# Spreading a batch's four value gathers over six units of a paged attention loop

## The chip, the cores and the metric

The kernel runs on one core of a Trainium2 chip. The time is device time of one execution, in microseconds; three runs of the kernel before give 2389.03, 2390.1 and 2392.03, median 2390.1. A profile was taken of one further execution.

## The reference

Four layers are added to `x` one after another (64 batches of 32 rows and 512 columns; the attention reads the rows as tokens): a product with a weight chosen by condition, a base weight with adapters of rank 16, an attention over a paged cache, and again a product by condition. The change lies in the third:

```python
x = x + _L0_cond_ref(x, itok_B_0_15, L0_cond_weights)
x = x + _L1_cond_ref(x, itok_B_6_15, ...)
x = x + _L2_cond_ref(x, ..., L2_cond_k_cache, L2_cond_v_cache, itok_Bx16_0_63, itok_B_207_1644)
x = x + _L3_cond_ref(x, L3_cond_weights, itok_B_0_15)
# in L2, for each batch: 32 query heads, 8 key heads of 128, 16 pages of 32 rows plus 32 own rows
kc = k_cache[block_table].reshape(bsz, L, HK, D)        # L = 512
vc = v_cache[block_table].reshape(bsz, L, HK, D)
k_all, v_all = concatenate([kc, k]), concatenate([vc, v])
scores = where(valid, einsum('bqhd,bkhd->bhqk', q, k_all) * SCALE, -1e30)
o = einsum('bhqk,bkhd->bqhd', softmax(scores), v_all)
return einsum('bse,de->bsd', o.reshape(bsz, seqlen, HQ * D), Wo)
```

## The kernel before

The attention is a loop over 512 units. A unit is one key head of one batch with its four query heads, which are stacked to 128 rows of queries against 544 keys. Eight units make a batch, 32 units (four batches) a group, and there are 16 groups. Every engine runs its own `step(g, u)` for each unit, u from 0 to 31, and the steps are staggered by semaphores.

PE, in step u, in this order: `turn_own` (u a multiple of 4), `score` of unit u+2 (six matmuls, L1209), `turn_p` of unit u (four transposes, L1092; at multiples of 4 it comes after `values`), a part of `out_proj` of the finished group (only in steps 30, 31 and 0 to 5, L1260), and `values` of unit u-1 (four products of the values with the turned probabilities, L1241, and at the last of four units the own rows, L1252). Products in fp32r are made of three: high by high, high by low, low by high.

The split of keys and queries into high and low parts is shared. ACT makes `k_hi` of unit u+4 (L715). DVE makes the first 11 of 17 slots of `k_lo`, POOL the rest (both through `k_low`, L284). POOL also makes `q_hi` (L549) and `q_lo` (L551). POOL's `split_q(n + 4)` waits until PE has scored unit n+2 (`s_qk`), as it overwrites the buffer of that unit; PE's `score` waits for `s_klo` (DVE) and `s_qp` (POOL). DVE further takes the masked maximum (L975), and normalises the probabilities (L986, L987); ACT takes the exponentials (L721) and moves the turned probabilities out of PSUM (L765).

Values come from the cache in HBM by gathers. `gather_v` (L514) is an indirect DMA issued by POOL: it fetches 128 rows of 4 KB, that is 512 KB, into one of four parts of a batch's value buffer. There are two such buffers, `v_sb[0]` and `v_sb[1]`, used by alternate batches. POOL's `step` issues the gathers of batch g*4+k+2 with (u - 10) = 8k + m, m from 0 to 3: gather m in step 10 + 8k + m, behind the `split_q` of that step. At m = 0 it first waits until the batch that used the buffer is finished (`s_po`), and copies the next batch's indices (L511). With k = -1 these are steps 2 to 5, with k = 0, 1 and 2 steps 10 to 13, 18 to 21 and 26 to 29. The first group issues batch 1's gathers in steps 2 to 5 by a line of its own. All four gathers of a buffer add to `s_v`; PE's `values` waits for 64 on it at the batch's first unit, thus in step 17 for gathers of steps 10 to 13, in step 25 for those of 18 to 21, in step 1 of the next group for those of 26 to 29, and in step 9 for those of 2 to 5.

SP issues the other loads in a fixed order per batch: own keys and queries (L359, L361) once `s_qp` says that POOL has split the buffer's last unit, then sixteen pages of K of 128 KB (L354) once `s_klo` says it for DVE, then the own values (L366), then the store of the outputs.

Of the kernel before, what the change touches and what calls it, by code (L numbers as in the profile page):

```python
# [28 lines left out]
B, C, T = 64, 32, 512  # L29
# [7 lines left out]
BT = P // C  # L37
# [13 lines left out]

WO_AT = {UG - 2: 0, UG - 1: 2, 0: 4, 1: 6, 2: 8, 3: 11, 4: 14, 5: H2}
LOW = 11
WO_SPLIT = 8

SCALE = 1.0 / float(np.sqrt(D))
# [10 lines left out]
def ge(eng, sem, val):  # L67

    if not isinstance(val, int) or val > 0:
        eng.wait_ge(sem, val)  # L70


def build(nc, x, cond_row, id_row, bt_row, idx_pages, seq_tok, seq_all, w0, w3, wb, bias,
# [3 lines left out]
    with ctx:  # L77
# [203 lines left out]
        def k_low(engine, b, h, u, slots):  # L281

            lo, hi = (k[u % 2].rearrange("p (s t) -> p s t", t=PSIZE)[:, slots, :] for k in (k_lo, k_hi))
            return engine.tensor_tensor(lo, k_sb[b][:, slots, h, :], hi.bitcast(F32), ALU.subtract)  # L284
# [199 lines left out]
        @block.gpsimd  # L484
        def _(pool):
            PL = [mybir.EngineType.Pool]
            pool.wait_ge(s_ids, 32)
            pool.wait_ge(s_la, 16)

            def pick(i, j):  # L490

                ge(pool, s_hmm, i * 4 - 3 + j)
                _, rows = nc.values_load_multi_w_load_instructions(
                    ids[0:1, bass.ds(i * 16 + 4 * j, BT)], engines=PL, min_val=0, max_val=LORAS - 1)
                for b in range(BT):
                    nc.gpsimd.tensor_copy(a4[j][:, :, b * RANK:(b + 1) * RANK],
                                          la_sb[:, bass.ds(rows[b], 1), :].rearrange("p a (c r) -> p (a c) r", c=HC))\
                        .then_inc(s_pick[j], 1)

            for j in range(4):  # L500
                pick(0, j)
            with pool.Fori(1, NT // 4) as i:
                for j in range(4):
                    pick(i, j)

            pool.wait_ge(s_x2T, NT)
            for j in range(4):
                pool.wait_ge(s_x2st[j], 16 * (NT // 4))
            def next_idx(b, k):

                nc.gpsimd.tensor_copy(idx[k][:], idx_all[:, bass.ds(b * 4, 4)]).then_inc(s_idx, 1)  # L511

            def gather_v(k, par, m):
                nc.gpsimd.indirect_dma_start(  # L514
                    out=v_sb[par][:, m, :], out_offset=None, in_=v_cache,
                    in_offset=bass.IndirectOffsetOnAxis(ap=idx[k][:, m:m + 1], axis=0)).then_inc(s_v[par], 16)

            nc.gpsimd.memset(ones[:], 1.0).then_inc(s_ones, 1)
            pool.wait_ge(s_ones, 5)
            pool.wait_ge(s_idx0, 1)  # L520
            next_idx(0, 0)
            next_idx(1, 1)
            next_idx(2, 2)
            pool.wait_ge(s_idx, 2)
            for m in range(4):
                gather_v(0, 0, m)


            def add_halves(e, t):
                pool.wait_ge(s_rot, e * NT + t + 1)  # L530
                ge(pool, s_tq, e * NT + t - 3)
                qv = qr_sb[t % 4].rearrange("p (h d) -> p h d", h=4)
                for lo, hi in ((0, HD), (HD, 0)):
                    nc.gpsimd.tensor_tensor(qv[:, :, lo:lo + HD], t1_sb[t % 2][:, :, lo:lo + HD],  # L534
                                            t2_sb[t % 2][:, :, hi:hi + HD], ALU.add).then_inc(s_qr, 1)

            for t in range(NT):
                add_halves(0, t)
            with pool.Fori(1, QKB - 1) as e:
                for t in range(NT):  # L540
                    add_halves(e, t)
            def split_q(n, u, pair):

                b, h = u // HK % 2, u % HK
                if h == 0:
                    pool.wait_ge(s_k[b], pair * KLOAD + KLOAD)
                ge(pool, s_qk, n - 1)
                q = q_sb[b][:, h * P:(h + 1) * P]
                nc.gpsimd.tensor_tensor(q_hi[u % 2], q, ones[:], ALU.mult).then_inc(s_qhi, 1)  # L549
                pool.wait_ge(s_qhi, n + 1)  # L550
                nc.gpsimd.tensor_tensor(q_lo[u % 2], q, q_hi[u % 2].bitcast(F32), ALU.subtract)  # L551
                pool.wait_ge(s_khi, n + 1)
                k_low(nc.gpsimd, b, h, u, slice(LOW, NPP + 1)).then_inc(s_qp, 1)

            def step(g, u):
                n = g * UG + u
                fixed = isinstance(n, int)
                if not (fixed and n + 4 >= NU):
                    split_q(n + 4, u + 4, g * 2 + (u + 4) // (2 * HK))

                k, m = (u - 10) // HK, (u - 10) % HK
                if m < 4 and not (fixed and not 2 <= g * BT + k + 2 < B):
                    if m == 0:
                        b = g * BT + (k + 2)
                        pool.wait_ge(s_idx, b + 1)
                        pool.wait_ge(s_po, g * (2 * BT) + 2 * (k + 1))
                        next_idx(b + 1, (k + 3) % 4)
                    gather_v((k + 2) % 4, k % 2, m)

            for t in range(NT):  # L570
                add_halves(QKB - 1, t)
                if t in (NT - 4, NT - 2):
                    u = (t - (NT - 4)) // 2
                    split_q(u, u, 0)
            for u in range(2, 4):
                split_q(u, u, 0)
            for u in range(ROT):
                step(0, u)
                if 2 <= u < 6:
                    gather_v(1, 1, u - 2)  # L580
            with pool.Fori(0, NT - 1) as g:
                for u in range(ROT, UG):
                    step(g, u)
                for u in range(ROT):
                    step(g + 1, u)
            for u in range(ROT, UG):
                step(NT - 1, u)
            pool.wait_ge(s_po, NU // 4)
            for i in range(2):
                nc.gpsimd.memset(bd3[i], 0.0).then_inc(s_zero3, 1)  # L590
# [3 lines left out]
        def _(act):  # L594
# [149 lines left out]
            def split_wo(half, h, raw):  # L744

                if h == 0:
                    act.wait_ge(s_wo_in, 16 * half + 16)
                at = slice(h * T, (h + 1) * T)
                nc.scalar.copy(wo_hi[:, at], raw[:, at]).then_inc(s_wohi, 1)

            def step(g, u):
                n = g * UG + u
                fixed = isinstance(n, int)
                if u % 4 == 0 and not (fixed and n == 0):
                    own_turned(g, u)
                if not (fixed and n + 4 >= NU):
                    split_k(n + 4, u + 4, g * 2 + (u + 4) // (2 * HK))
                if u % 4 == 0:
                    if not (fixed and n + 2 >= NU):
                        exps(n + 2, u + 2)  # L760
                    if not (fixed and n == 0):
                        out_heads(g, u)
                act.wait_ge(s_ta, n + 1)
                ge(act, s_pv, n - 1)
                nc.scalar.copy(pT_sb[u % 2], pT).then_inc(s_evA, 1)  # L765
                if u % 4 and not (fixed and n + 2 >= NU):
                    exps(n + 2, u + 2)
# [16 lines left out]
            for u in range(ROT):  # L784
                step(0, u)
                if 0 <= u - WO_SPLIT < H2:
                    split_wo(0, u - WO_SPLIT, wo_raw)
            with act.Fori(0, NT - 1) as g:
# [31 lines left out]
        def _(dve):  # L820
# [142 lines left out]
            def split_k(n, u):  # L963

                b, h = u // HK % 2, u % HK
                dve.wait_ge(s_khi, n + 1)
                k_low(nc.vector, b, h, u, slice(0, LOW)).then_inc(s_klo, 1)

# [32 lines left out]
            def split_wo(half, h, lo, raw):  # L1001

                dve.wait_ge(s_wohi, half * H2 + h + 1)
                at = slice(h * T, (h + 1) * T)
                nc.vector.tensor_tensor(lo[:, at], raw[:, at], wo_hi[:, at].bitcast(F32), ALU.subtract).then_inc(s_wolo, 1)
# [33 lines left out]
            for u in range(ROT):  # L1039
# [3 lines left out]
                step(0, u, None)  # L1043
                if 0 <= u - WO_SPLIT < H2:
                    split_wo(0, u - WO_SPLIT, wo_lo, wo_raw)
            with dve.Fori(0, NT - 1) as g:
# [347 lines left out]
```

## Time and profile before

| | us |
|---|---|
| median of three runs | 2390.1 |
| lowest, highest | 2389.03, 2392.03 |
| the profiled execution | 2394.14 |
| its span | 2392.4 |
| PE, DVE, ACT, POOL busy | 2312.0, 1760.8, 1535.2, 1395.5 |
| 256 gathers (L514), POOL busy | 270.0 |
| wait of POOL's `q_hi` for PE's scores | 229.1 |

The span is the time from the first to the last instruction of the profiled execution. Busy time of PE is that of pipelined matmuls, so 97% doesn't say that it works at its peak. A row of the timeline is: start in us from the span's start, length, engine, line, operation, tile written and tiles read, shape, count, and in brackets idle time before it with what released it. A gather's row is the time that POOL spends on issuing it; the data move later, on queue q0.

### The profile page before, as it was taken

Reading aid. Unit: us, or ns where it says so; the run is one execution under the profiler, and the core shown is the slowest. Engines: PE = TensorE matmul, PEld = TensorE weight load, DVE = VectorE, ACT = ScalarE, POOL = GpSimd, SP = SyncE. Lnnn points to the kernel's source line nnn. Section 1 sums busy time; section 2 is a strip of 40 time slices with the busy share of each in tenths; the row PEclk is TensorE's granted clock in tenths of the full one; section 3 lists DMA queues with packets and bytes.
Section 4 is the critical chain, followed back from the end, with each engine's and each line's share of the span. In section 5 each row is a group of like instructions: output and inputs, shape, how many; then the busy total and the mean of one; then the engine's idle time right before and its main releaser. Section 6 shows DMA issues by size and latency. Waiting matters only on the chain.

```text
span 2392.4 us, 58277 instructions
## 1 busy us (share of the span) xinstructions
PE 2312.0 (97%) x15392; PEld 2010.2 (84%) x15392; DVE 1760.8 (74%) x5422; ACT 1535.2 (64%) x4221; POOL 1395.5 (58%) x2249
## 2 busy tenths in 40 slices
PE   8999999999998899999999999999999999998999
PEld 5778888888887788888888888888888888887777
DVE  4434777777778887887887887887887887886232
ACT  4324666666667777777777777777777777775221
POOL 1003454444447777877877877877877877872000
PEclk9999999999998999999999999999999999999999
DMA  4335333333337777777767777777767777775332
GB/s 164 95 110 163 102 98 102 111 106 102 97 115 257 221 224 239 253 228 237 255 223 241 253 228 237 255 223 242 252 220 245 253 223 241 253 221 194 110 132 101
DMA packets 347959, 455.96 MB, mean 191 GB/s; under 512 B 34506, under 2 KB 280842, under 8 KB 343695
## 3 DMA queue, kind: packets, MB, share of 16 engines
q1 hardware_dynamic: 308398, 315.83, 41.9%
q0 software_dynamic: 36864, 134.23, 16.9%
q10 hardware_dynamic: 2528, 4.29, 0.5%
q14 instruction: 141, 1.15, 0.2%
q8 instruction: 28, 0.46, 0.1%
HBM read 374.53 MB, written 79.69 MB: 190 GB/s over the span
## 4 chain that ended last, share of the span: by engine, by line
PE 48%; DVE 23%; issue 19%; ACT 5%; POOL 3%; DMA 1%; DVEq 0%; ACTq 0%; POOLq 0%; SPq 0%
PE S L1168 11%; PE oP L1168 11%; DVE regC L987 8%; PE S L1260 7%; DVE k_lo L284 7%; PE oP L1241 3%; PE oP L1092 3%; DVE regC L986 3%; PE S L1209 3%; PE bank L1092 2%; PE oP L1122 2%; ACT regC L721 2%; PE bank L1260 2%; DVE nmx L975 1%; DVE rinv L981 1%
## 5 line engine op out<-in xcount | busy, mean ns | idle before, releaser
L1241 PE MATMUL oP<-regC,regK 128*128 128x128 f32 x4096 | 541.2, 275 | 0.1
L1241 PEld LDWEIGHTS oP<-regC,regK 128*128 128x128 f32 x4096 | 507.2, 192 | 9.6 <-issue 0.3
L975 DVE CUSTOM_DVE_ANT_0 regC<-S,mask 128x544 f32<-128x544 f32 x512 | 368.1, 719 | 187.9 <-issue 185.7
L715 ACT CAST k_hi<-regK 128x544 fp32r<-128x544 f32 x512 | 331.3, 647 | 210.5 <-PE S L1209 184.1
L721 ACT ACTIVATE regC<-regC,nmx 128x544 f32<-128x544 f32 x512 | 384.9, 752 | 58.8 <-DVE nmx L975 49.8
L534 POOL TENSOR_TENSOR regC<-regC 128x256 f32<-128x256 f32 x320 | 244.3, 784 | 278.3 <-DVE regC L944 278.3
L549 POOL TENSOR_TENSOR q_hi<-regC,ones 128x128 fp32r<-128x128 f32 x512 | 262.3, 512 | 233.8 <-PE S L1209 229.1
L1092 PE MATMUL bank<-ident,regC 128*128 128x128 f32 x2048 | 321.1, 279 | 26.9 <-ACT regC L765 21.0
L284 POOL TENSOR_TENSOR k_lo<-regK,k_hi 128x192 fp32r<-128x192 f32 x512 | 341.4, 667 | 3.3 <-ACT k_hi L715 3.3
L987 DVE TENSOR_SCALAR regC<-regC,rinv 128x512 f32<-128x512 f32 x512 | 337.8, 660 | 0.0
L284 DVE TENSOR_TENSOR k_lo<-regK,k_hi 128x352 fp32r<-128x352 f32 x512 | 328.2, 641 | 2.9 <-ACT k_hi L715 2.9
L765 ACT COPY regC<-bank 128x512 f32<-128x512 f32 x512 | 298.6, 583 | 23.7 <-PE bank L1092 19.3
L514 POOL DMA_INDIRECT regK<-v_cache,idx x256 | 270.0, 1055 | 39.2 <-issue 15.4
L551 POOL TENSOR_TENSOR q_lo<-regC,q_hi 128x128 fp32r<-128x128 f32 x512 | 264.6, 517 | 40.1
L1092 PEld LDWEIGHTS bank<-ident,regC 128*128 128x128 f32 x2048 | 226.8, 140 | 71.8 <-issue 49.6
L1209 PE MATMUL S<-k_hi,q_hi 128*128 128x288 f32 (+1 forms) x1024 | 254.5, 330 | 26.9 <-POOL k_lo L284 20.5
L1209 PE MATMUL S<-k_hi,q_lo 128*128 128x288 f32 (+1 forms) x1024 | 212.9, 289 | 0.0
L1209 PE MATMUL S<-k_lo,q_hi 128*128 128x288 f32 (+1 forms) x1024 | 212.2, 289 | 0.0
L1209 PEld LDWEIGHTS S<-k_hi,q_hi 128*128 128x128 f32 x1024 | 155.2, 192 | 49.3 <-issue 42.8
L986 DVE TENSOR_SCALAR regC<-regC,rinv 128x32 f32<-128x32 f32 x512 | 183.8, 359 | 0.1
L944 DVE SCALAR_TENSOR_TENSOR regC<-oP,rstd,regK 128x128 f32<-128x128 f32 x640 | 173.1, 343 | 8.5
L944 DVE SCALAR_TENSOR_TENSOR regC<-S,rstd,regK 128x128 f32<-128x128 f32 x640 | 172.8, 343 | 8.2
(137 smaller groups left out, 4468.9 us busy)
## 6 DMA issues: line engine op xcount, KB each, us to landing
regK<-kT_cache SPq DMA_DIRECT2D x1024, 128.0 KB
qkT_d<-regC SPq DMA_DIRECT2D x160, 256.0 KB, 2.3
regC<-qkT_d SPq DMA_DIRECT2D x64, 512.0 KB
oT_d<-regC SPq DMA_DIRECT2D x64, 256.0 KB
regK<-oT_d SPq DMA_DIRECT2D x16, 1024.0 KB, 5.0
regC<-wqk SPq DMA_DIRECT2D x10, 1024.0 KB, 5.2
v_d<-regC SPq DMA_DIRECT2D x32, 256.0 KB, 2.3
regK<-qkT_d SPq DMA_DIRECT2D x64, 128.0 KB
```

What stands on the lines that cost most here:

```text
L284: return engine.tensor_tensor(lo, k_sb[b][:, slots, h, :], hi.bitcast(F32), ALU.subtract)
L514: nc.gpsimd.indirect_dma_start(out=v_sb[par][:, m, :], out_offset=None, in_=v_cache, in_offset=bass.IndirectOffsetOnAxis(ap=idx[k][:, m:m ...
L715: nc.scalar.copy(k_hi[u % 2].rearrange("p (s t) -> p s t", t=PSIZE), k_sb[b][:, :, h, :]).then_inc(s_khi, 1)
L721: nc.scalar.activation(p, p, ACT.Exp, bias=nmx[:, u % 4:u % 4 + 1], scale=-1.0, accum_out=rs[:, u % 4:u % 4 + 1]).then_inc(s_exp, 1)
L765: nc.scalar.copy(pT_sb[u % 2], pT).then_inc(s_evA, 1)
L944: last = nc.vector.scalar_tensor_tensor(out=dst[t % 2][:, h, :], in0=bank[t % 4][:, h * D:(h + 1) * D], scalar=rstd[:, t % 4, h:h + 1], in ...
L975: nc.vector.tensor_tensor_reduce(out=p_sb[u % 4], in0=scores, in1=mask[u // HK % 2][:], scale=-SCALE, scalar=3e38, op0=ALU.add, op1=ALU.mi ...
L987: nc.vector.tensor_scalar(p[:, 0:L], p[:, 0:L], rinv[:, j:j + 1], None, ALU.mult).then_inc(s_p, 1)
L1092: last = nc.tensor.transpose(dst[:, c * P:(c + 1) * P], src[:, c * P:(c + 1) * P], ident[:])
L1168: last = nc.tensor.matmul(bank[t % 4], a[:, c, rows], w[k][:, cols], start=(c == 0 and m == 0), stop=(c == HC - 1 and m == 2))
L1209: last = nc.tensor.matmul(scores[:, at], q[u % 2], k[u % 2][:, at], start=(m == 0), stop=(m == 2))
L1241: last = nc.tensor.matmul(oP[:, j * 512:j * 512 + P], v_sb[b][:, m, u % HK * D:(u % HK + 1) * D], pT_sb[u % 2][:, m * P:(m + 1) * P], star ...
```

## The change

POOL's `step` issues a batch's gathers in the third, fifth, sixth and eighth of eight steps in place of the third to the sixth. Gather 0 with its waits and its index copy stays; gather 1 comes one step later, gather 2 one, gather 3 two. The line of the first group for batch 1 isn't changed.

```diff
 WO_AT = {UG - 2: 0, UG - 1: 2, 0: 4, 1: 6, 2: 8, 3: 11, 4: 14, 5: H2}
 LOW = 11
+GATHER_AT = {0: 0, 2: 1, 3: 2, 5: 3}
 WO_SPLIT = 8
...
                 k, m = (u - 10) // HK, (u - 10) % HK
-                if m < 4 and not (fixed and not 2 <= g * BT + k + 2 < B):
+                if m in GATHER_AT and not (fixed and not 2 <= g * BT + k + 2 < B):
                     if m == 0:
                         b = g * BT + (k + 2)
                         pool.wait_ge(s_idx, b + 1)
                         pool.wait_ge(s_po, g * (2 * BT) + 2 * (k + 1))
                         next_idx(b + 1, (k + 3) % 4)
-                    gather_v((k + 2) % 4, k % 2, m)
+                    gather_v((k + 2) % 4, k % 2, GATHER_AT[m])
```

## Rows read from the trace of the kernel before

**Rows 1.** The page's first part: busy us, share of the span, instructions.

```profile
PE 2312.0 (97%) x15392; PEld 2010.2 (84%) x15392; DVE 1760.8 (74%) x5422; ACT 1535.2 (64%) x4221; POOL 1395.5 (58%) x2249
```

**Rows 2.** Waits of PE over the span: us in total, times, longest.

```profile
PE S L1209 <- POOL k_lo L284: 20.5, 35, 0.7
```

**Rows 3.** Timeline of PE, 1402 to 1426: scores S(9) to S(18), two `values`.

```profile
1402.51 0.49 PE L1209 MATMUL S<-k_hi,q_hi 128*128 128x288 f32 x2
...
1404.24 1.06 PE L1241 MATMUL oP<-regC,regK 128*128 128x128 f32 x8
1405.05 0.50 PE L1209 MATMUL S<-k_hi,q_hi 128*128 128x288 f32 x2
...
1409.67 0.49 PE L1209 MATMUL S<-k_hi,q_hi 128*128 128x288 f32 x2
...
1412.33 0.49 PE L1209 MATMUL S<-k_hi,q_hi 128*128 128x288 f32 x2
...
1414.08 1.06 PE L1241 MATMUL oP<-regC,regK 128*128 128x128 f32 x8
...
1420.30 0.49 PE L1209 MATMUL S<-k_hi,q_hi 128*128 128x288 f32 x2 [0.53 <-POOL k_lo L284]
...
1422.96 0.50 PE L1209 MATMUL S<-k_hi,q_hi 128*128 128x288 f32 x2
...
1425.33 0.49 PE L1209 MATMUL S<-k_hi,q_hi 128*128 128x288 f32 x2
```

**Rows 4.** Timeline of POOL, 1406 to 1422, starts of steps 10 to 16, gathers.

```profile
1406.13 0.46 POOL L549 TENSOR_TENSOR q_hi<-regC,ones 128x128 fp32r<-128x128 f32 x1 [0.99 <-PE S L1209]
...
1409.30 0.47 POOL L549 TENSOR_TENSOR q_hi<-regC,ones 128x128 fp32r<-128x128 f32 x1
...
1411.51 0.98 POOL L514 DMA_INDIRECT regK<-v_cache,idx  x1
1412.51 0.68 POOL L549 TENSOR_TENSOR q_hi<-regC,ones 128x128 fp32r<-128x128 f32 x1
...
1414.42 0.98 POOL L514 DMA_INDIRECT regK<-v_cache,idx  x1
1415.43 0.61 POOL L549 TENSOR_TENSOR q_hi<-regC,ones 128x128 fp32r<-128x128 f32 x1
...
1417.28 1.13 POOL L514 DMA_INDIRECT regK<-v_cache,idx  x1
1418.42 0.48 POOL L549 TENSOR_TENSOR q_hi<-regC,ones 128x128 fp32r<-128x128 f32 x1
...
1420.16 0.74 POOL L549 TENSOR_TENSOR q_hi<-regC,ones 128x128 fp32r<-128x128 f32 x1
...
1421.95 0.45 POOL L549 TENSOR_TENSOR q_hi<-regC,ones 128x128 fp32r<-128x128 f32 x1
```

**Rows 5.** DMA, 1409.9 to 1412.1 (gather 0, started 1408.17): packets, MB, share.

```profile
q0 software_dynamic: 144, 0.52, 80.0%
```

**Rows 6.** The same, 1419.4 to 1421.6 (gather 3, and SP's queue q1).

```profile
q0 software_dynamic: 144, 0.52, 59.9%
q1 hardware_dynamic: 275, 0.25, 33.1%
```

**Rows 7.** Timeline of POOL in steps 5 and 7: gather 3 of batch 29, step 7.

```profile
1395.71 0.99 POOL L514 DMA_INDIRECT regK<-v_cache,idx  x1
...
1398.81 0.45 POOL L549 TENSOR_TENSOR q_hi<-regC,ones 128x128 fp32r<-128x128 f32 x1
...
1399.75 0.60 POOL L284 TENSOR_TENSOR k_lo<-regK,k_hi 128x192 fp32r<-128x192 f32 x1
```

**Rows 8.** DMA packets of q0, 1395.7 to 1401.3 (gather 3 of batch 29).

```profile
q0 software_dynamic: 145, 0.52, 34.3%
```

**Rows 9.** Timeline of POOL: gather 3 of batch 32, step 29.

```profile
1458.01 1.14 POOL L514 DMA_INDIRECT regK<-v_cache,idx  x1
```

**Rows 10.** Timeline of PE: the first `values` of batch 32, step 1.

```profile
1469.64 1.05 PE L1241 MATMUL oP<-regC,regK 128*128 128x128 f32 x8
```

## The prediction

> **What bounds the kernel now.** I read the page first: PE is busy 97% of the span [rows 1], so time is lost or won only where PE's next instruction is late. Then the list of PE's waits: for `k_lo` from POOL it waits 20.5 us, in 35 places of up to 0.7 us [rows 2]. Then the timeline of PE across batch 30's gathers, to see where these places are. I call "step u" one turn of `step` on every engine, counted within a group of 32, and S(u) the start of its score matmuls on PE. In step u PE scores unit u+2, and POOL, once that score has ended, splits unit u+4. In [rows 3] S(9), S(10), S(12) and S(13) are 1402.51, 1405.05, 1409.67 and 1412.33: four steps take 9.82 us. By that rhythm S(14) is 1414.87, S(16) 1419.49, S(17) 1422.15 and S(18) 1424.69. The rows show 1420.30 for S(16) (0.53 idle, released by POOL's `k_lo`), 1422.96 and 1425.33. So POOL's lateness costs PE 0.64 us of the 20.28 us of this batch.
>
> The timeline of POOL says why. On time, POOL starts a step 1.08 us after S(u) (1405.05 on PE, 1406.13 on POOL). The first gather step takes 3.17 us (to 1409.30), the next three 3.21, 2.92 and 2.99 [rows 4], against 2.46 us for a mean step of PE. POOL begins step 14 at 1418.42, where 1414.87 + 1.08 = 1415.95 was due: 2.5 us late, more than its lead of two steps hides. There are two such batches in each of the 16 groups, those whose first gather is in step 10 or 18, and 32 x 0.64 = 20.5 us is the sum that the list of waits has. In the other two the gathers lie in steps 26 to 29 and 2 to 5, and `out_proj` (steps 30 to 5) slows PE there, so POOL keeps up.
>
> **The change, part by part.** Nothing is added or removed: the same 256 gathers, the same index copies. Gather 0 and its waits stay in the third step of the batch's turn; gathers 1, 2 and 3 move 1, 1 and 2 steps later (steps 12, 13 and 15 for batch 30). They are issued by POOL between two `split_q`, so each passes one or two of those on POOL's own queue; nothing of SP's queue is passed, whose page loads hang on `s_qp` and `s_klo`.
>
> (a) *POOL's lateness.* A step that begins late takes, without its gather, 2.21, 1.91, 1.85, 1.74 and 1.79 us (from `q_hi` to whatever follows `k_lo`; mean 1.90), and a gather 1.00, 1.01 and 1.14 (mean 1.05) [rows 4]. A step can be as short as 1.54 (1398.81 to 1400.35) [rows 7]. In the new order POOL starts step 11 at 1409.30 as now, step 12 at 1411.20, step 13 at 1414.15, step 14 at 1417.10 and step 15 at 1419.00. The `k_lo` that S(16) wants is then ready at 1419.0, before 1419.49, and that of S(17) at 1420.8, before 1422.15. The 0.64 us go, 20.5 us in all.
>
> (b) *The last gather's landing.* `values` of a batch's first unit waits for all four gathers. That is in step 17, and all else on PE is queued behind it, the next score first. Now gather 3 starts at 1417.28, and its 144 packets are through by 1421.6, 4.3 us later [rows 6], before step 17 begins. In the new order it starts at 1419.00 + 1.90 = 1420.90 and lands at 1425.2. PE wants it at S(17) + 1.75 = 1423.90 (the 1.75 is 1412.33 to 1414.08 in the same kind of step [rows 3]). So PE waits 1.3 us: S(18) comes at 1426.0 in place of 1425.33, **0.66 us later than now**, the gain of (a) already counted. For 32 batches that is 21.1 us lost. The landing has two ends: gather 0, which runs alone, is through 3.9 us after its start [rows 5], and the fourth gather of batch 29 takes up to 5.6 [rows 7, 8]. I take 4.3, because that one ran beside K's pages (the 275 packets of SP's queue in [rows 6]), as the moved one will. The late step's ends are 1.54 and 2.21, and I take the mean of the late ones, since POOL is late from step 11 on in the new order too.
>
> The Trainium skill ("DMA: Bandwidth & Descriptors", section "Anatomy of one DMA — SWDGE (gpsimd) path") fits a DMA issued from GpSimd by 2.0 us and its bytes at 436 GB/s; for 0.52 MB that makes 3.2 us as an estimate. The trace disagrees: the gather with no other packets beside it took 3.9 [rows 5].
>
> (c) *The batch of steps 2 to 5* (batch 29 here). Now its gather 3 goes out in step 5, at 1395.71 [rows 7], and PE wants it in step 9, at 1404.24 [rows 3]. POOL's lateness costs PE nothing here, so there is nothing to win. In the new order gather 3 goes out behind step 7's `k_lo`, at 1400.5, and lands at 1404.8 (with 4.3) or 1406.1 (with 5.6): a wait of 0.56, at most 1.9. There are 15 such batches (the first group keeps its own order for it): 8.4 us.
>
> (d) *The batch of steps 26 to 29* (batch 32). Its gather 3 starts at 1458.01 and is wanted at 1469.64 [rows 9, 10]: 11.6 us. It moves by two steps, one of them with `out_proj`, some 4 us by the pace of (a) and (c); over 7 are left, more than any landing here. Nothing.
>
> Sum: 21.1 + 8.4 = 29.5 us. The profiled execution took 2394.1 us (its span is 2392.4), which makes 2423.6; the median of the runs lies 4.0 below the profiled execution, so **2420 us**.
>
> **Rivals.**
> 1. *The last gather is in time* (faster). If POOL's steps took 1.54 each, gather 3 would start at 1409.30 + 5 x 1.54 + 2 x 1.05 = 1419.1 and with the shorter landing be there at 1423.0, before 1423.90. Then (a) is a gain, 20.5 us less 15 x 0.16 for (c): 18 us, 2372 us. It decides at a mean step of 1.72, where a landing of 4.3 leaves no change, and no late step in [rows 4] is below 1.74.
> 2. *The landing is that of the lone gather, the steps as now*: 3.9 in place of 4.3. PE waits 0.9, so 0.26 x 32 + 0.16 x 15 = 11 us, 2401 us.
> 3. *The landing is shorter than any row has it*, so that PE waits 0.2 us in (b) and not at all in (c): 0.44 x 32 = 14 us gained, 2376 us. That needs a landing of 3.2, and the shortest in the rows is 3.9. The 3.2 of the page named in (b) would do this.
> 4. *The late gather meets a backlog of page loads* (slower still). With 5.6 in place of 4.3 all 47 waits grow by 1.3 us: 29.5 + 61 = 91 us, 2481; half of it, 2450, is likelier. For it speaks batch 29's fourth gather [rows 7, 8]; against it, that gather 3 of batch 30 moved its 0.52 MB in 2.2 us beside pages, as gather 0 did alone [rows 5, 6].
> 5. *One wait takes the place of the other*, of the same size: within 5 us of now. It needs mean steps near 1.72.
>
> **How the numbers follow.** My forecast, a wait for values larger than what POOL gives back (2405 to 2440): 0.52. Rivals 1 to 5: 0.16, 0.08, 0.04, 0.10, 0.10. A measurement of this kernel can't tell less than some 0.2% (5 us) from no change. Slower: 0.52 + 0.08 + 0.10 = 0.70; faster: 0.16 + 0.04 = 0.20; within 0.2%: 0.10. The range 2375 to 2448 holds the forecast, its bounds, and what lies between; it leaves out half of rival 1 and half of rival 4.
>
> **What would show it.** In the profile after, PE's wait for POOL's `k_lo` falls from 20.5 to under 3 us (a). A new wait of PE or of its weight load stands at `oP` L1241, once in three batches of four, about 1.3, 1.3 and 0.6 us, released by a DMA or called "issue" (b, c), and none for the batch of (d). Gather 3 starts some 15.9 us after S(10) and lands 4.3 later. The eight steps 10 to 17 take 20.9 us in place of 20.3. I am wrong at (a) if gather 3 starts under 15 us after S(10), since POOL's steps were then less disturbed than I say; wrong at (b) if it starts at 15.9 and `values` doesn't wait, since then the landing or PE's rhythm isn't what I take it for.

## The result, and the profile after

The changed kernel takes 2592.7 us (median of six runs, 2589.6 to 2602.6) against 2390.2 us of the kernel before on the same chip, a ratio of 1.0854 with a 95% interval of 1.0832 to 1.0875. The forecast was 2420 us, with 2448 as its upper end: the sign is right, the size is out by a factor of seven. The profiled execution took 2590.3 us, its span is 2588.5. (Lines are one higher than before, because of the new line 54: L1242 is what was L1241.)

The waits of PE over the span answer to [rows 2]. Columns are the tile and line that waited, what released it, us in total, times, the longest.

```profile
PE oP L1242 <- DMA regK<-v_cache,idx: 149.0, 45, 4.4
...
PE S L1210 <- POOL k_lo L285: 3.9, 8, 0.6
```

The wait for POOL fell from 20.5 to 3.9 us, close to what step (a) of the prediction has (under 3). A new one came for the gathers, 45 times with a mean of 3.3 us, where 47 with a mean of 1.1 us were forecast. The timeline of PE in step 17, for batch 30 as in [rows 3], shows two things:

```profile
1510.22 0.49 PE L1210 MATMUL S<-k_hi,q_hi 128*128 128x288 f32 x2
...
1511.31 0.63 PE L1093 MATMUL bank<-ident,regC 128*128 128x128 f32 x4
1515.12 1.36 PE L1242 MATMUL oP<-regC,regK 128*128 128x128 f32 x8 [3.19 <-DMA regK<-v_cache,idx]
1516.13 0.80 PE L1210 MATMUL S<-k_hi,q_hi 128*128 128x288 f32 x2
1516.73 0.66 PE L1210 MATMUL S<-k_lo,q_hi 128*128 128x288 f32 x2
...
1519.72 0.50 PE L1210 MATMUL S<-k_hi,q_hi 128*128 128x288 f32 x2
```

`values` begins 4.90 us after the score (1510.22 to 1515.12), where 1.75 is the rhythm and 3.05 was forecast. And the work after the wait is itself slower: from score to score (1516.13 to 1519.72) it takes 3.59 us. The kernel before takes 2.09 for the same step, from S(18) at 1425.33 [rows 3] to S(19):

```profile
1427.42 0.50 PE L1209 MATMUL S<-k_hi,q_hi 128*128 128x288 f32 x2
```

The table of stretches says why; its columns are the stretch, its length, busy time and count of PE, PE's weight loads, DVE, ACT and POOL, the granted clock, the DMA engines' share and GB/s:

```profile
1511.00:1512.00 1.00, 0.84 (x6) 0.42 (x4) 0.74 (x4) 0.84 (x3) 1.00 (x3) 1.00 0.81 148
...
1514.00:1515.00 1.00, 0.00 (x0) 0.00 (x0) 0.00 (x0) 0.00 (x0) 0.00 (x0) 1.00 1.04 363
1515.00:1516.00 1.00, 0.88 (x7) 0.88 (x8) 0.00 (x0) 0.00 (x0) 0.00 (x0) 0.97 1.06 364
1516.00:1517.00 1.00, 1.00 (x7) 1.00 (x6) 0.00 (x0) 0.00 (x0) 0.00 (x0) 0.50 0.83 224
1517.00:1518.00 1.00, 1.00 (x6) 1.00 (x6) 0.11 (x2) 0.12 (x1) 0.07 (x1) 0.50 0.97 255
1518.00:1519.00 1.00, 1.00 (x7) 1.00 (x6) 1.00 (x4) 0.79 (x2) 0.92 (x3) 0.50 0.60 184
```

PE stood still for 3.2 us, and from 1516 on its granted clock is 0.50, that is 1.2 in place of 2.4 GHz, for some three microseconds.

Where the 3.2 us come from, the gather's own rows show. Gather 3 goes out here (timeline of POOL):

```profile
1508.80 0.98 POOL L515 DMA_INDIRECT regK<-v_cache,idx  x1
```

and its 144 packets are moved between 1510.6 and 1514.7 (DMA queues in that stretch: packets, MB, share of 16 engines):

```profile
q0 software_dynamic: 144, 0.52, 50.3%
q1 hardware_dynamic: 661, 0.60, 43.7%
```

They are through 5.9 us after the start. Beside them SP's queue moved 0.60 MB; in [rows 6] it was 0.25 MB, and 4.3 us. SP's K pages are in full flow here, 4 us old when the gather goes out:

```profile
1504.74 8.71 SPq L355 DMA_DIRECT2D regK<-kT_cache  x16
```

Averaged over groups 2 to 12 of the trace, a group of four batches went from 90.0 to 103.5 us. The steps 9, 17 and 25, in which `values` waits, grew by 3.4, 4.3 and 4.5 us, and the three steps behind them, at half clock, by 1.1 to 1.4 each: together 16.0. Steps 13 to 15 and 21 to 23, where POOL had been late, gave back 1.0 and 1.1.

### The profile page after: what moved, and what is told of

Its sections match the earlier page's. It is cut to its first block, busy times and chain, and to the rows that moved or that the text cites. A ratio compares the mean times of both kernels' runs of the same rounds, so it can differ in the third digit from the quotient of the medians.

```text
span 2588.5 us, 58277 instructions
## 1 busy us (share of the span) xinstructions
PE 2381.6 (92%) x15392; PEld 2082.3 (80%) x15392; DVE 1779.4 (69%) x5422; ACT 1538.8 (59%) x4221; POOL 1400.0 (54%) x2249
## 4 chain that ended last, share of the span: by engine, by line
PE 59%; POOL 14%; issue 13%; DMA 6%; DVE 6%; ACT 2%; POOLq 0%; ACTq 0%; SPq 0%; DVEq 0%
PE S L1169 10%; PE oP L1169 10%; PE oP L1242 8%; PE S L1261 7%; PE S L1210 6%; PE bank L1261 6%; DMA regK<-v_cache,idx 5%; PE bank L1093 4%; POOL k_lo L285 4%; POOL q_lo L552 4%; POOL q_hi L550 3%; PE oP L1093 3%; POOL regK L515 3%; PE oP L1123 2%; DVE regC L988 2%
## 5 line engine op out<-in xcount | busy, mean ns | idle before, releaser
L1242 PE MATMUL oP<-regC,regK 128*128 128x128 f32 x4096 | 584.5, 289 | 149.1 <-DMA regK<-v_cache,idx 149.0
L1242 PEld LDWEIGHTS oP<-regC,regK 128*128 128x128 f32 x4096 | 545.5, 204 | 169.0 <-DMA regK<-v_cache,idx 104.3
L550 POOL TENSOR_TENSOR q_hi<-regC,ones 128x128 fp32r<-128x128 f32 x512 | 242.9, 474 | 427.8 <-PE S L1210 422.9
L988 DVE TENSOR_SCALAR regC<-regC,rinv 128x512 f32<-128x512 f32 x512 | 366.5, 716 | 0.0
L285 POOL TENSOR_TENSOR k_lo<-regK,k_hi 128x192 fp32r<-128x192 f32 x512 | 355.7, 695 | 3.6 <-ACT k_hi L716 3.6
L1093 PE MATMUL bank<-ident,regC 128*128 128x128 f32 x2048 | 334.9, 288 | 22.3 <-ACT regC L766 14.3
L552 POOL TENSOR_TENSOR q_lo<-regC,q_hi 128x128 fp32r<-128x128 f32 x512 | 278.2, 543 | 40.1
L1093 PEld LDWEIGHTS bank<-ident,regC 128*128 128x128 f32 x2048 | 240.2, 146 | 64.1 <-issue 44.9
L1210 PE MATMUL S<-k_hi,q_hi 128*128 128x288 f32 (+1 forms) x1024 | 266.7, 343 | 9.0 <-DVE nmx L976 4.6
L1210 PEld LDWEIGHTS S<-k_hi,q_hi 128*128 128x128 f32 x1024 | 164.9, 203 | 20.6 <-issue 15.0
```

Of the source, the lines that this page charges most:

```text
L988: nc.vector.tensor_scalar(p[:, 0:L], p[:, 0:L], rinv[:, j:j + 1], None, ALU.mult).then_inc(s_p, 1)
L1093: last = nc.tensor.transpose(dst[:, c * P:(c + 1) * P], src[:, c * P:(c + 1) * P], ident[:])
L1210: last = nc.tensor.matmul(scores[:, at], q[u % 2], k[u % 2][:, at], start=(m == 0), stop=(m == 2))
L1242: last = nc.tensor.matmul(oP[:, j * 512:j * 512 + P], v_sb[b][:, m, u % HK * D:(u % HK + 1) * D], pT_sb[u % 2][:, m * P:(m + 1) * P], star ...
```

## The experiments

**Gather 3 alone in the eighth unit.** The first question was whether the last gather carries the loss, or the spreading of the others.

```diff
-GATHER_AT = {0: 0, 2: 1, 3: 2, 5: 3}
+GATHER_AT = {0: 0, 1: 1, 2: 2, 5: 3}
```

> The changed kernel with gathers 1 and 2 put back to their old steps; gather 3 alone stays in the batch's eighth unit. Theory A (the whole loss hangs on where the last gather lands): gather 3 starts as before about 1.1 us ahead of the score of the step that waits for it, values waits 3.1 to 3.7 us in three batches of four, and PE's clock falls after each: 2575 to 2605 us. Rival B (the loss comes from spreading as such, from gathers 1 and 2 lying between splits of POOL): with two of three moves undone, no more than 2500 us.

It took 2532.0 us, ratio 1.060 (1.056 to 1.064). Neither theory's range holds it. Most of the loss is there with the last gather alone (142 of 202 us), so B falls; but 60 us depend on the other two. The trace says how. Gather 3 starts 1.2 us ahead of S(17), as in the changed kernel, but lands after 4.7 us in the batches of step 10 and 5.1 in those of step 18 (means over 11 groups), not 5.9 and 6.1. The page bytes moved beside it are 0.38 and 0.45 MB, not 0.64. Gather 2, one step sooner here, isn't moved amid the pages: in these batches it lands after 3.8 to 3.9 us with at most 0.02 MB of pages beside it, in the changed kernel after 4.4 to 4.5 us with 0.21 to 0.26 MB. So it seems to leave a shorter queue of pages for gather 3 to meet; that last link I only argue, no run isolates it.

**Gather 3 in the seventh unit.**

```diff
-GATHER_AT = {0: 0, 2: 1, 3: 2, 5: 3}
+GATHER_AT = {0: 0, 2: 1, 3: 2, 4: 3}
```

> The changed kernel with gather 3 in the seventh unit in place of the eighth (third, fifth, sixth, seventh). Theory A (landing of 5.9 us beside K's page loads, 0.5 us more until PE goes on): gather 3 starts some 2.3 to 3 us earlier; its packets still meet the page loads, so it lands after 4.8 to 5.5, and values waits 0 to 1 us: 2375 to 2440 us. Rival C (a landing of 4.3 as I predicted, and the loss has another cause): no wait for values and the 20 us of POOL's lateness won: 2368 to 2375 us.

2482.3 us, ratio 1.039 (1.032 to 1.046): both missed. Gather 3 did start sooner, 3.0 us ahead of S(17), but it took 6.1 to 6.3 us to land, no less than the 5.9 to 6.05 of the eighth unit, and `values` began 3.6 to 3.8 us after the score in place of 5.3 to 5.4. The start came 1.9 us sooner than in the changed kernel, and the wait shrank by 1.5 to 1.8.

**Small page loads.** To see what K's pages do to the gather, all page loads of batches from 2 on move one partition (`load_pages` gets an argument `rows`, which is P where none is given); the scores are then not the reference's:

```diff
-                    sp.dma_start(k_sb[par][:, first + n, :, :].rearrange("p h t -> p (h t)"),
-                                 kT_cache[bass.ds(pages[n], 1)].rearrange("a p n -> p (a n)")).then_inc(s_k[par], 16)
+                    sp.dma_start(k_sb[par][0:rows, first + n, :, :].rearrange("p h t -> p (h t)"),
+                                 kT_cache[bass.ds(pages[n], 1), 0:rows].rearrange("a p n -> p (a n)")).then_inc(s_k[par], 16)
...
-                        load_pages(b, k % 2)
+                        load_pages(b, k % 2, rows=1)
```

> The changed kernel, but from batch 2 on each page load of K moves one partition in place of 128, so 1 KB in place of 128 KB; the scores of those batches are therefore not the reference's. Theory A (the late gather is slow because K's pages stand ahead of it on the DMA engines): its packets are through 3.8 to 4.1 us after its start in place of 5.9, values waits about 1.5 us in place of 3.3, 2440 to 2500 us. Rival D (a gather behind others of its own queue is slow by itself): 5.5 us or more and 2560 to 2600 us.

2453.8 us, ratio 1.027 (1.024 to 1.030), in the range of A; D falls. Gather 3 lands after 3.85 to 3.97 us in all batches. The same edit on the kernel before is the control:

> The kernel before, but from batch 2 on each page load of K moves one partition in place of 128, so the scores of those batches are not the reference's. It is the control to the same edit in the changed kernel. Theory A: the page loads cost the old order nothing, since its last gather lands 2.5 us before it is wanted: 2383 to 2392 us. Rival H (the page loads slow the whole loop, so that what the edit won in the changed kernel has nothing to do with the gather): 2300 to 2360 us.

2390.6 us, ratio 1.000 (0.999 to 1.001), so H falls. The pages cost the old order nothing and the new one 139 us.

**Filling PE's wait.** To part the wait from the half clock behind it, idle products stand ahead of the wait, so that PE isn't still:

```diff
                 if u % HK == 0:
+                    if u and not isinstance(n, int):
+                        for _ in range(17):
+                            nc.tensor.matmul(oP[:, 3 * 512 + P:4 * 512], wo_hi[:, 0:P], wo_hi[:, 0:3 * P], start=True, stop=True)
```

> The changed kernel with 17 idle products of 128 by 384 put on PE ahead of the wait for values in the three batches of four that wait, from group 1 to 14 and into 15: 2.8 us of work that fits into a wait of 3.1 to 3.7. Theory E (after the wait PE runs at half clock for some 3 us, which costs 1.4 to 1.9 us a batch): the granted clock stays at 1.00 and the time falls by 55 to 80 us, to 2510 to 2535 us. Rival F (the slow steps after the wait are the pipeline filling again, not the clock): 2585 to 2600 us.

2548.1 us, ratio 1.067 (1.063 to 1.070): with 3.0 us more work per waiting batch (17 products, one every 0.174 us) the kernel is 45 us quicker than the changed one. The clock of the span is 0.995, against 0.962. Batch 30 again, the timeline of PE and two stretches with the columns of before (L1245 is `values` here):

```profile
1489.02 3.22 PE L1235 MATMUL oP<-wo_hi 128*128 128x384 f32 x17
1492.73 1.16 PE L1245 MATMUL oP<-regC,regK 128*128 128x128 f32 x8 [0.49 <-DMA regK<-v_cache,idx]
1493.64 0.50 PE L1210 MATMUL S<-k_hi,q_hi 128*128 128x288 f32 x2
...
1495.73 0.49 PE L1210 MATMUL S<-k_hi,q_hi 128*128 128x288 f32 x2
```

```profile
1493.00:1494.00 1.00, 1.00 (x11) 1.00 (x11) 0.00 (x0) 0.00 (x0) 0.00 (x0) 1.00 0.85 276
1494.00:1495.00 1.00, 1.00 (x11) 1.00 (x10) 0.31 (x2) 0.32 (x1) 0.28 (x1) 1.00 0.50 156
```

Just behind the wait DVE, ACT and POOL have nothing to do, as in the changed kernel, but the steps there take 2.08 us again in the mean, in place of 3.2 to 3.5. So F falls and E holds in kind, though the gain is 45 us and not 55 to 80, and the time 13 us over its range. One reason is in the trace: at half clock PE gives POOL time to catch up, so that in the changed kernel gather 3 starts 1.1 us ahead of S(17); with the clock kept it starts only 0.75 ahead.

**Both edits at once.** This leaves the late start alone. The waits are shorter with small pages, so fewer idle products stand ahead of them: 3 in the batch of steps 2 to 5, 10 in the two that follow.

> The changed kernel with both edits: page loads of K of one partition (scores of batches from 2 on are not the reference's), and idle products on PE ahead of the wait, 3 of them (0.5 us) in a group's batch of steps 2 to 5 and 10 (1.65 us) in the two that follow. What is left is the late start of gather 3 with a landing of 3.9 and 0.4 to 0.6 until PE goes on, without pages beside it and without half clock. Theory A: 0.6 us a batch in 15 batches, 1.9 less 0.65 in 32: 40 to 55 us over the kernel before, 2432 to 2446 us, granted clock 0.99 or more. Rival K (a fourth cause is at work, or the clock has cost nothing there): 2450 to 2460 us as without the filling.

2442.8 us, ratio 1.022 (1.020 to 1.024), within A's range; the clock is 0.995. With this run the loss has a table (medians; the kernel before at 2390):

| | K's pages whole | K's pages of one partition |
|---|---|---|
| PE idle in the wait | 2593 | 2454 |
| wait filled | 2548 | 2443 |

A late start without pages and without half clock costs 52 us (2443 less 2390); a few of them may be the idle products' own, since in most of these waits PE goes from the last of them to `values` without a pause. The pages add 105 (2548 less 2443). The half clock adds 45 where the waits are long, and 11 where they are short.

The run also shows what was wrong with my start of gather 3. Timeline of POOL for the same batch, here with S(10) at 1424.75:

```profile
1429.01 0.47 POOL L550 TENSOR_TENSOR q_hi<-regC,ones 128x128 fp32r<-128x128 f32 x1
1431.03 0.46 POOL L550 TENSOR_TENSOR q_hi<-regC,ones 128x128 fp32r<-128x128 f32 x1
...
1433.21 0.98 POOL L515 DMA_INDIRECT regK<-v_cache,idx  x1
1434.21 0.47 POOL L550 TENSOR_TENSOR q_hi<-regC,ones 128x128 fp32r<-128x128 f32 x1
...
1436.29 0.98 POOL L515 DMA_INDIRECT regK<-v_cache,idx  x1
1437.29 0.51 POOL L550 TENSOR_TENSOR q_hi<-regC,ones 128x128 fp32r<-128x128 f32 x1
...
1439.01 0.46 POOL L550 TENSOR_TENSOR q_hi<-regC,ones 128x128 fp32r<-128x128 f32 x1
...
1441.05 0.97 POOL L515 DMA_INDIRECT regK<-v_cache,idx  x1
```

The five steps take 2.02, 2.18, 2.08, 1.72 and 2.04 us, mean 2.01, where I had 1.90 from the steps of the old order. Gather 3 starts 16.3 us after S(10), not 15.85.

And PE begins `values` not when the last packet is through, but later. The changed kernel's rows above show it: the last packet is through at 1514.7, and `values`, for which PE had stood idle 3.19 us, starts at 1515.12. In the means by batch of the runs in which PE stood idle it is 0.4 to 0.8 us between the last packet and the first product. I had left it out.

**Page loads sooner.** The other way to part gather and pages keeps all the work: SP reads the page numbers before its waits instead of between wait and load (`page_numbers` holds the reading that stood at the top of `load_pages`).

```diff
+                        pages = page_numbers(b)
                         sp.wait_ge(s_qp, g * UG + HK * (k + 1))
                         load_own(b, k % 2)
                         sp.wait_ge(s_klo, g * UG + HK * (k + 1))
-                        load_pages(b, k % 2)
+                        load_pages(b, k % 2, pages=pages)
```

> The changed kernel with all its work, but SP reads the sixteen page numbers of K before it waits, so the page loads go out some 5 us sooner and are nearly through when gather 3 starts. Theory A: gather 3 lands after 4.0 to 4.8 us in place of 5.9, values waits 1.5 to 2.3 us, 2450 to 2510 us. Rival D (the last gather is slow by itself): 2580 to 2600 us.

2540.4 us, ratio 1.062 (1.060 to 1.065): 52 us quicker than the changed kernel, but short of the range. In the batches of steps 10 and 18 the pages still flow when gather 3 starts (the last is issued 0.2 us ahead of it), and it takes 5.8 and 5.7 us. In those of steps 2 to 5 the last page was issued 3.6 us before it starts. There the same gather, in the same kernel, lands after 3.8 us on the mean. For batch 29, issued at 1463.8, the packets of both queues from 1465.5 to 1467.4, and PE:

```profile
q0 software_dynamic: 144, 0.52, 80.4%
q1 hardware_dynamic: 18, 0.01, 2.0%
```

```profile
1467.74 1.16 PE L1246 MATMUL oP<-regC,regK 128*128 128x128 f32 x8
```

`values` begins there 2.07 us after its score in the mean, where the changed kernel has 4.80 and the rhythm 1.72: the wait is nearly gone. So it is the pages beside the gather, with no work left out.

> The kernel before with the page numbers of K read before the wait, as in the run of the changed kernel. Theory A: now it is the old order whose last gather meets the page loads in full flow; it lands after 5 to 6 us in place of 4.3, still 0 to 1 us before it is wanted, so 2385 to 2400 us, and the gap between the two orders shrinks from 200 us to 60 to 115. Rival D: both orders stay where they were, the gap stays 200.

2394.8 us, ratio 1.0014 (1.0005 to 1.0024). Gather 3 of the old order now lands after 6.0 to 6.5 us in place of 4.2 to 5.4, and it costs 3 us in all, since even in the two tighter batches 0.9 us still lie between its last packet and `values`. The time is in A's range. The gap between the orders is 146 us in place of 202; A's range for it was too low by 30, for the reason just told.

**A pause without a later end.** If POOL's lateness is worth 20 us and a late last gather is ruin, the pause should be made by starting sooner. The buffer is free a unit earlier, as `s_po` for it comes in step 8.

```diff
-GATHER_AT = {0: 0, 2: 1, 3: 2, 5: 3}
+GATHER_AT = {0: 0, 1: 1, 3: 2, 4: 3}
...
-                k, m = (u - 10) // HK, (u - 10) % HK
+                k, m = (u - 9) // HK, (u - 9) % HK
```

> The gathers start one unit sooner (the batch whose buffer they take is finished by then) and have a pause after the second: second, third, fifth and sixth unit of eight, so gather 3 stays where it was in the kernel before. Theory A (POOL's lateness costs 0.64 to 0.8 us in two batches of four and a last gather that goes out in the sixth unit is in time): POOL's wait of PE falls from 20.5 to under 5 us, no wait for values, 2365 to 2373 us. Rival G (POOL's lateness is covered by something else, DVE's chain or ACT's, once it goes): 2383 to 2390 us.

2407.2 us, ratio 1.0059 (1.0042 to 1.0076): 0.6% slower, and both ranges missed. PE's wait for POOL is down to 3.6 us and the batch of step 10 takes 19.7 us in place of 20.3, as A has it. But that of step 18 takes 22.0 in place of 20.4, all of it in one step, 21. The waits of ACT have a new row:

```profile
ACT k_hi L716 <- DMA regK<-kT_cache: 33.1, 14, 6.7
```

The gathers that begin in step 17 now share the DMA engines with the pages of the batch that starts at unit 24, and `split_k` for it, in step 20, finds them late. Two runs test this. The first has both edits, the sooner start and the page numbers read ahead:

> The order with the gathers in units two, three, five and six together with the page numbers of K read ahead, so that the page loads go out 5 us sooner. Theory I (that order lost its gain because its first gathers delayed K's pages, for which ACT then waited 33 us): ACT's wait for K's pages is gone, the second batch of a group falls from 22.0 to 19.7 to 19.9 us; gathers beside pages in full flow take 6.0 to 6.5 us and values waits 0 to 0.3 us: 2364 to 2380 us. Rival J (gather 3 is now too late by half a microsecond or more and PE falls to half clock): 2390 to 2430 us.

2381.1 us, ratio 0.9955 (0.9938 to 0.9971). ACT's wait for pages is gone from the list, and the batch of step 18 takes 20.0 us. That is the fastest kernel of the study, 10 us under the one before. Its time lies 1 us over the range of I: gathers 2 and 3 land after 5.8 to 6.6 us, and 0.1 to 0.2 us of wait and 10.9 us for POOL's `k_lo` are left.

The second moves only a group's batch of step 10, so that no gather of the next batch goes out sooner than before and meets those pages:

```diff
                 k, m = (u - 10) // HK, (u - 10) % HK
+                if 9 <= u < 14:
+                    k, m = 0, {9: 0, 10: 1, 12: 2, 13: 3}.get(u, 4)
```

> The kernel before; only in a group's first full batch (16 of 64) do the gathers go out in steps 9, 10, 12 and 13 in place of 10 to 13. Theory A with I: this batch falls from 20.3 to 19.7 us as it did in the run with all batches early, the others stay, 16 x 0.6 = 9 us: 2378 to 2384 us. Rival G (what is won there is given back in the next batch, whose K pages or gathers then come too late): 2387 to 2395 us.

2383.7 us, ratio 0.9976 (0.9965 to 0.9987), within A's range. The batch takes 19.7 us, the others are as before, and PE's wait for POOL is 12.8 in place of 20.5 us.

## Why the prediction was wrong in size

*What bounds the kernel, (a)*: held. PE's wait for POOL's `k_lo` fell from 20.5 to 3.9 us, where I had under 3, and some 0.6 us a batch come back when nothing else is in the way (in early_one 20.3 to 19.7 in 16 batches, 7 us in the time).

*(b), the wait for values*: the mechanism held, in the three batches that I named and not in the fourth. Its size failed in three terms.

1. **The landing, 4.3 us.** This is the step that failed. I took it from gather 3 of the old order, "because that one ran beside K's pages, as the moved one will". But that gather was issued 0.6 us before the page loads began, and met their first 0.2 MB (mean of 11 groups); the moved one is issued 3.8 us after they began and meets 0.64 MB. It takes 5.9 us. The prediction says that "nothing of SP's queue is passed"; in time the gather went from ahead of the page loads to behind them. Means over 11 groups, by the page bytes that moved between the gather's first and last packet:

| page bytes moved beside gather 3 | through after |
|---|---|
| under 0.03 MB | 3.9 us |
| 0.20 MB (before, step 10) | 4.3 us |
| 0.38 MB (only_last8, step 10) | 4.7 us |
| 0.45 MB (only_last8, step 18) | 5.1 us |
| 0.64 MB (changed) | 5.9 us |

 Not all means lie on this line. With the page numbers read ahead (before_pages_early) gather 3 takes 6.0 to 6.5 us beside 0.43 to 0.52 MB; there its first packet comes 3.2 to 3.8 us after the start, in place of 1.7 to 2.1 in the rows of the table, and only 0.5 to 1.0 us after the last one of gather 2, which itself took 5.9 to 6.2 us beside the pages. So a gather ahead of it in the same queue, itself delayed by pages, seems to count too; no run isolates that. The gather's packets aren't slower (4 KB in 206 ns in the mean, 200 with small pages); others stand between them. The Trainium skill ("DMA: Bandwidth & Descriptors", section "Queues, rings and completion order") says that an engine takes its queues in turn, a packet from each. The trace agrees as far as both queues move side by side, with near equal bytes (0.52 and 0.60 MB in the same 4.1 us); that it is one packet from each in turn its rows don't show, as 661 of pages stand there beside 144 of the gather. I had the 5.6 us of batch 29 [rows 7, 8] as rival 4 and gave it a tenth, since one fast gather beside pages spoke against it. The row that said so was there: 275 packets of pages beside it, where sixteen loads make some 2000. Pages cost 105 us, of which my 4.3 in place of 3.9 had held some 19.

2. **What lies between the last packet and `values`**, 0.4 to 0.7 us in the changed kernel, wasn't in the sum, and **the start of gather 3** was 0.45 us later than I had it, as POOL's steps took 2.0 us in the new order. Together they explain the late start's 52 us: with a landing of 3.9 my working gives 11 us (rival 2), and 47 x 0.5 + 32 x 0.45 = 38 us more make 49. (In the changed kernel itself gather 3 starts 1.1 us ahead of S(17), near the 1.25 of the forecast, because the half clock holds PE back too.) For 47 waits a term of half a microsecond is 24 us; a landing should have been taken up to the waiting engine's first instruction. The Trainium skill's same page (section "Anatomy of one DMA — SWDGE (gpsimd) path") counts the completion into a DMA's fixed cost and warns that it is long; my row of packets ended before it.

3. **The half clock**, 45 us, wasn't in the sum at all. I looked at PE's clock before (0.994 of full) and took it for given, though the change puts an idle stretch of PE where there had been none.

*(c)*: the same, 3.1 us of wait and 0.3 us of half clock in the step, 1.1 in the next, against 0.56. *(d)*: held, step 1 takes 3.75 us before and after; its slack fell from 7.4 to 1.5 us though, more than the 4 us of the move, because its landing grew too (4.2 to 6.2 us).

*Rivals*: rival 4 was the one that came true, in double its size: 91 us for a landing of 5.6, plus the two terms that I had not seen. Rivals 1, 3 and 5 fall by all runs.

What stays open: why gather 3 in the seventh unit takes no less (6.1 to 6.3 us) than in the eighth, though it starts 1.8 us after the pages begin and not 3.8, with no more page bytes beside it (0.59 to 0.62 MB). Its first packet comes later there (2.35 us after the start, against 2.06). That gather 2 still holds the queue doesn't fit the trace: its last packet is through 1.1 us before. Single gathers spread from 5.5 to 7.6 us, so the difference itself may be small; no run tested it.

## What to carry to other kernels

A transfer that is moved later costs nothing only until its slack is gone; price the landing in the traffic of its new place, up to the first instruction of the engine that waits, not by the row of its old place. When a change makes PE stand still for some microseconds at regular intervals, look whether its clock falls, and add what that takes from the work behind each wait (here 45 us for 47 waits of 3.3). Here the pause in a chain of issues was better made by starting sooner (7 and 10 us gained, some 15 lost where it pushed K's pages back) than by ending later (202 lost); one has to ask whose transfers the earlier ones push back.

## What the runs showed of the hardware

An indirect gather of 128 rows of 4 KB took 3.8 to 4.1 us (means by batch) from its instruction's start to its last packet with next to no pages beside it, and 4.2 to 6.6 beside a stream of 128 KB loads from SP, more the more of them it met; PE went on 0.4 to 0.8 us later still. PE idle for 3.2 us was followed by about 3 us at a granted clock of 0.50, and with idle products in the wait the clock stayed at 1.00. What I had expected least is the last: PE doing 3.0 us of useless work in each wait made the kernel 45 us faster.
